# A region of DRAM for each expert's rows, the experts between superblocks 4 and 5, and one maximum over two banks

## The reference

```python
x  = L0_attn_x                                   # (2, 2048, 128)
xn = layernorm(x)
# attention branch, for each batch
s = xn @ W_spin.T + b_spin
scores = (s @ W_J.T) @ s.T / sqrt(128)           # 2048 x 2048
local = softmax(scores) @ s
attn = tanh(beta * (s + mean(s) @ W_global.T + local))
# expert branch, for each token
logits = xn @ Wg.T + bg                          # 16 experts
rw = softmax(top 2 of the logits)
gate, up = (xn @ Wgu[e] + bgu[e])[::2], [1::2]   # gate <= 7, up within +-7
out = sum over the 2 experts of rw * ((up + 1) * gate * sigmoid(1.702 * gate)) @ Wd[e] + bd[e]
result = x + attn + out
```

## Time and profile before

| | us |
|---|---|
| median of 3 runs | 362.35 (361.89 to 365.35) |
| profiled execution | 362.15 |
| its span, first to last instruction | 360.4 |
| busy: PE / DVE / ACT / POOL | 324.9 / 309.9 / 256.8 / 203.7 |
| clock granted to TensorE, mean | 0.981 of 2.4 GHz |

### The profile page before, as it was taken

One profiled execution on the slowest core, in us unless ns is written; L12 is line 12 of the kernel. 1 busy time (PEld: TensorE's weight loads), 2 busy tenths in 40 slices (PEclk: granted clock), 3 DMA queues, 4 the chain that ended last, 5 costly groups with the idle time before them and its releaser, 6 DMA issues.

```text
span 360.4 us, 5972 instructions
## 1 busy us (share of the span) xinstructions
PE 324.9 (90%) x1778; PEld 271.9 (75%) x1779; DVE 309.9 (86%) x630; ACT 256.8 (71%) x509; POOL 203.7 (57%) x271
## 2 busy tenths in 40 slices
PE   1878999998999999999978999999899998989980
PEld 1666788776777778888768999999788786867750
DVE  5988979999978999999769999888878999987855
ACT  2754777876699797687646988888787586578751
POOL 4276851325777777777113444534137777777760
PEclk9978999999999999999999999999999999999996
DMA  5999710000111211212222877765543354555551
GB/s 148 325 332 340 282 35 0 1 31 7 51 51 54 80 46 53 90 51 82 74 87 75 241 222 229 235 207 178 178 117 107 104 164 123 131 145 133 133 126 34
DMA packets 41359, 45.97 MB, mean 128 GB/s; under 512 B 3770, under 2 KB 33082, under 8 KB 41330
## 3 DMA queue, kind: packets, MB, share of 16 engines
q1 hardware_dynamic: 36162, 32.94, 29.1%
q0 software_dynamic: 5168, 12.67, 12.4%
HBM read 23.46 MB, written 22.12 MB: 126 GB/s over the span
## 4 chain that ended last, share of the span: by engine, by line
PE 40%; DVE 22%; POOL 19%; issue 8%; ACT 5%; DMA 4%; POOLq 0%; SPq 0%; ACTq 0%; DVEq 0%
POOL made L547 9%; POOL gy L547 8%; PE PS L556 8%; PE PS L558 8%; PE PS L557 8%; DVE mx L1121 6%; DVE pl L1106 5%; PE PS L609 4%; PE PS L661 2%; PE PS L786 2%; PE PS L771 2%; DVE stats L1077 2%; DMA xy<-slots_x 1%; PE PS L788 1%; PE PS L791 1%
## 5 line engine op out<-in xcount | busy, mean ns | idle before, releaser
L921 ACT ACTIVATE PS<-PS 128x512 f32<-128x512 f32 x128 | 74.8, 585 | 42.8 <-PE PS L558 41.2
L1106 DVE TENSOR_TENSOR pl<-PS,ph 128x512 fp32r<-128x512 f32 x128 | 87.7, 685 | 14.1 <-ACT ph L932 13.5
L1121 DVE TENSOR_REDUCE mx<-PS 128x1 f32<-128x512 f32 x128 | 84.3, 682 | 6.0 <-PE PS L609 6.0
L932 ACT ACTIVATE ph<-PS 128x512 fp32r<-128x512 f32 x128 | 76.5, 598 | 12.1 <-PE PS L558 0.8
L517 POOL DMA_INDIRECT slots_x<-xn,posu x64 | 63.0, 985 | 19.7 <-issue 17.1
L609 PE MATMUL PS<-xT,gq 128*128 128x512 f32 x128 | 49.5, 423 | 6.6 <-DVE mx L1121 6.3
L556 PE MATMUL PS<-gq,xT 128*128 128x512 f32 x128 | 52.4, 410 | 1.5 <-ACT gq L937 0.8
L556 PE MATMUL PS<-ph,rows 128*128 128x512 f32 x128 | 51.5, 402 | 1.8 <-DVE pl L1106 1.8
L558 PE MATMUL PS<-gq,xT 128*128 128x512 f32 x128 | 50.1, 391 | 0.0
L558 PE MATMUL PS<-ph,rows 128*128 128x512 f32 x128 | 50.1, 391 | 0.0
L557 PE MATMUL PS<-pl,rows 128*128 128x512 f32 x128 | 50.0, 391 | 0.0
(11 more groups left out here) (199 smaller groups left out, 682.8 us busy)
## 6 DMA issues: line engine op xcount, KB each, us to landing
slots_y<-yr SPq DMA_DIRECT2D x20, 512.0 KB, 3.1
slots_x<-xs SPq DMA_DIRECT2D x1, 5120.0 KB, 22.0
xy<-slots_x SPq DMA_DIRECT2D x20, 256.0 KB, 3.0
xn<-in_L_attn_x SPq DMA_DIRECT2D x8, 256.0 KB, 5.5
w_f<-in_L_ffn_Wgu SPq DMA_DIRECT2D x1, 2048.0 KB, 12.8
late<-in_L_ffn_Wgu SPq DMA_DIRECT2D x1, 2048.0 KB, 18.3
xs<-in_L_attn_x SPq DMA_DIRECT2D x8, 256.0 KB, 3.5
out_y<-made SPq DMA_DIRECT2D x7, 256.0 KB, 3.3
```

The costliest lines, as they stand in the source:

```text
L921: A(S[:, n % 3], S[:, n % 3], ACT.Exp).then_inc(exp_done, 1)
L932: A(ph[:, i % RING], S[:, n % 3], ACT.Copy).then_inc(s_hi, 1)
L1106: v.tensor_tensor(dst, S[:, n % 3], high.bitcast(F32), ALU.subtract).then_inc(s_lo, 1)
L1121: v.tensor_reduce(mx4[:, a, c:c + 1], MX[:, n % 2], AX.X, ALU.max).then_inc(mx_free, 1)
```

## The change

- Each expert has a region of its own in `slots_x` and `slots_y`, 33 tiles (`ETILES`), so a row number needs only the ranks within the tokens counted so far. Routing is done in two halves of 2048 tokens: choices, shares, `count_pairs`, `ranks`, `places` and the scatter of the first half, then of the second. `tile_list` then makes the list of the 80 tiles: first the whole tiles that the first half has filled, then the others.
- A row of `slots_x` has 129 numbers, the weight last; `xn` likewise. The column of ones in `xy` needs no restoring. Zeros are written only behind the regions and behind each expert's last row (16 transfers).
- SP loads and stores each of a group's four tiles with a transfer of its own, whose row it reads from the list `tile_of` (`rows_at`); its loop is written out. The buffers `xs` of the tokens now serve as `xy`.
- `MOE_AT` is 64: the experts stand between superblocks (numbered from 0) 3 and 4. `oT_part` goes.
- The maxima of superblocks 1 to 7 are made two products at a time (`maxima_pair`) into both banks of `MX`, and reduced by one instruction over 1024 numbers (`maximum_pair`), in two of three steps.
- `add_parts` moves from VectorE to POOL, behind the gathers of the next superblock.

The diff, cut to its core:

```diff
-    MOE_AT = 5 * TB - 4
+    MOE_AT = 4 * TB
+    ETILES = NT + 1
+    REGION = ETILES * P
+    ROWS = (NE * ETILES + NE) * P
...
-        GLOBAL_AT = {12: 0, 14: 1}
-        COUNT_AT = {16: 0, 17: 1}
+        GLOBAL_AT = {16: 0, 28: 1}
+        COUNT_AT = {13: 0, 19: 1}
...
+        def pair_at(j):
+            return 2 * (j // 3) + j % 3 if j < 12 and j % 3 < 2 else None
...
+                sp.wait_ge(pads_ready, 1)
+                for n in range(0, NE, 4):
+                    for row in rows_at(pad_i[0:1, n:n + 4]):
+                        sp.dma_start(slots_x[bass.ds(row, P)], zer[:]).then_inc(pads, 16)
...
-                    sp.dma_start(xy[:, u], slots_x_v[:, bass.ds(4 * g + 8, 4)]).then_inc(xg_in[u], 16)
+                def group_in(g):
+                    for a, row in enumerate(rows_at(tile_of[:, 1, 4 * g:4 * g + 4])):
+                        sp.dma_start(xy[:, g % 2, a], slots_x[bass.ds(row, P)]).then_inc(xg_in[g % 2], 16)
...
-                    sp.dma_start(slots_y_v[:, bass.ds(4 * g - 8, 4)], yr[:, u]).then_inc(y_out[u], 16)
+                    for a, row in enumerate(rows):
+                        sp.dma_start(slots_y[bass.ds(row, P)], yr[:, u, a].bitcast(U32)).then_inc(y_out[u], 16)
...
+                for g in range(2, NG + 2):
+                    if g + 2 <= NG - 3:
+                        rows_in(g + 2)
+                    if g == NG:
+                        sp.wait_ge(t_fill, rows_fill(NG - 1) + 1)
+                        sp.wait_ge(w_kept, NG)
+                        tokens_in(2)
+                    results_out(g)
                     if g < NG:
                         bias_in(g, g % 2)
...
+            def ranks_of(b):
+                pool.wait_ge(e_free, e_no["R", b] + 1)
+                g.tensor_tensor(KEY[:, of(b)], OH1[:, of(b)], RANK[:, of(b)], ALU.mult).then_inc(route_pool, 1)
+                g.tensor_tensor(PROD[:, of(b)], OH2[:, of(b)], RANK[:, of(b)], ALU.mult).then_inc(route_pool, 1)
...
+                        for t in range(part.start, part.stop):
+                            pool.indirect_dma_start(slots_x, bass.IndirectOffsetOnAxis(ap=posu[:, c, t:t + 1], axis=0),
+                                                    xn[:, t], None).then_inc(scat[b][2 if c else q], 16)
+                        if n == 0:
+                            list_consts()
+                            share_one(1)
+                            share_two(1)
+                        if n == 1:
+                            ranks_of(1)
...
+            def maxima_pair(k, q):
+                mx_bank(k, q)
+                a, c = q // 2, 2 * (q % 2)
+                for n in range(2):
+                    m = mm(MX[:, n], gq[:, k % 3, 0, a * P:(a + 1) * P], xT[k // CB][:, 0, 512 * (c + n):512 * (c + n) + 512],
+                           start=True, stop=True)
+                m.then_inc(mx_fill, 1)
...
+            def maximum_pair(k, q):
+                dve.wait_ge(mx_fill, mx_no(k, q) + 1)
+                v.tensor_reduce(mx4[:, q // 2, q % 2:q % 2 + 1], MX.rearrange("p b n -> p (b n)"), AX.X, ALU.max).then_inc(mx_free, 1)
...
+            def places(b):
+                for c in range(2):
+                    dve.wait_ge(route_pool, 4 * b + 3 + c + 2 * (1 - b))
+                    v.tensor_reduce(mk[:, 6, b * TB:b * TB + TB], (KEY, PROD)[c][:, b * TB:b * TB + TB], AX.X, ALU.add).then_inc(dchain, 1)
...
-            ROUTE_AT = {16: 4, 17: 5, 18: 6, 19: 7, 20: 8, 22: 9, 23: 10, 24: 11, 25: 12}
+            SHARE_AT = {13: 0, 22: 1}
+            RANKS_AT = {15: 0, 21: 1}
+            PLACES_AT = {16: 0, 23: 1}
+            LIST_AT = {25: 0, 26: 1, 28: 2, 29: 3}
```

More of the change, by code:

```diff
@@ L308, in _, with rows_at @@
                 sp.dma_start(b_d.rearrange("e (s n) -> e s n", s=2), b_rows[0:NE].bitcast(F32)).then_inc(bd_kept, 16)
+                def rows_at(which):
+                    _, rows = nc.values_load_multi_w_load_instructions(
+                        which, engines=(mybir.EngineType.SP,), min_val=0, max_val=ROWS - P,
+                        skip_runtime_bounds_check_because="the chip's own list of tiles")
+                    return rows
                 def tokens_in(k):
                     if k >= 2:
-                        sp.wait_ge(x_added, k - 1)
-                    sp.dma_start(xs[:, k % 2], x_v[k // CB][:, 4 * (k % CB):4 * (k % CB) + 4]).then_inc(ld_x[k], 16)
-                sp.wait_ge(zeroed, 16)
+                        sp.wait_ge(x_added, k - (k > 2))
+                    sp.dma_start(xs[:, k % 2, :, 0:D], x_v[k // CB][:, 4 * (k % CB):4 * (k % CB) + 4]).then_inc(ld_x[k], 16)
                 tokens_in(0)
@@ L571, in mx_bank @@
             def mx_bank(k, q):
[L572 to L579 removed]
+                if k and q < PAIRS:
+                    pe.wait_ge(mx_free, PAIRS * (k + 1) + q)
+                    if q == 0:
+                        pe.wait_ge(cr_done, k)
+                elif k == 0 and q >= 2:
+                    pe.wait_ge(mx_free, q - 1)
+                return MX[:, 0 if k else q % 2]
             pe.wait_ge(consts, 4)
@@ L702, in count_pairs @@
                 o = e_bank("R", k)
-                pe.wait_ge(oh_ready, 2)
-                mm(o, (onesb, tri)[k][:], ohb, start=True, stop=True).then_inc(e_fill, 1)
+                pe.wait_ge(oh_ready, k + 1)
+                for n in range(2):
+                    m = mm(o[:, n * TB * NE:(n + 1) * TB * NE], (onesb, tri)[n][:], ohb[:, k * TB * NE:(k + 1) * TB * NE],
+                           start=True, stop=True)
+                m.then_inc(e_fill, 1)
             def fields(k, h):
@@ L729, in step @@
                 if k + 1 < NSB:
-                    for q in maxima_at(j):
-                        maxima(k + 1, q, q // 4, q % 4)
+                    if pair_at(j) is not None:
+                        maxima_pair(k + 1, pair_at(j))
                     if j == 13:
@@ L973, in step @@
                     spins_out(*use)
-                if j == 2 and k:
+                if j == 2 and k and k != MOE_AT // TB:
                     values_hi(k - 1)
@@ L1307, in step @@
                 if k + 1 < NSB:
-                    for q in maxima_at(j):
-                        maximum(k + 1, q, q // 4, q % 4)
+                    if pair_at(j) is not None:
+                        maximum_pair(k + 1, pair_at(j))
                     if j == 12:
```

465 lines of the change are left out of this document (239 added, 226 removed).

## The result

The changed kernel takes **413.56 us** (median of 4 runs, 411.91 to 414.44), the kernel before 363.55 (4 runs, 361.89 to 365.35): a ratio of 1.137, with an interval of 1.130 to 1.144. It is slower by 50 us. I had forecast 398 with a range of 380 to 412, so direction and places were right and the loss was 14 us larger, just outside the range. The profiled run of the changed kernel took 411.91 us, its span is 409.8.

The account below looks back on a forecast made before the run. The kernel was taken as a chain of phases with TensorE or VectorE full (90 and 86% busy). From about 362 us, 12 + 2 + 1 + 27 + 2 - 4 - 4 = +36 gave 398 us, range 380 to 412.

Parts of the forecast that it names:

- The routing stall: Routing of the second half: POOL's rank products, queued behind sixteen scattered stores, hold up VectorE; +12 us, with +2 and +1 beside it.
- the wait: VectorE's step 23 idles 12 to 14 us for POOL's rank products behind the stores; +12 us, bounds +8 and +16.
- the clock: After VectorE's idle time in routing, TensorE runs at the lower clock for a while; +2 us, bounds 0 and +4.
- the list: Making the list of tiles takes 20 small VectorE operations in steps 25 to 29 instead of five; +1 us, 0 to +3.
- SP's transfers: Experts: SP issues eight transfers per group for two, so a group takes 5.4 us against 3.47; +27 us, +10 to +34.
- The rival that built on it, 371 us: Experts: SP's issues run hidden beside work and only the delay in routing stays; 371 us, chance 0.08.
- cheaper issues: Experts: SP's issues cost 0.40 to 0.47 us each with registers, +11 to +19 us; 382 to 390 us, chance 0.14.
- The low clock among the experts: Experts: TensorE idles and falls to the lower clock, a group's work taking about 6.4 us; 408 us, chance 0.15.
- Around the experts: Beside the experts: first gather starts four issues after the last result, tokens 2 load late; +2 us, 0 to +4.
- Pairs of maxima: Attention: one reduce of 1024 for two of 512 saves VectorE time, `add_parts` goes to POOL; -4 us, bounds -14 and +6.
- The end: Program's end: gathers finish before attention, so VectorE's last sums follow the last low part; -4 us, -4.6 to -2.

Follow-up runs that it names:

- experiment 1: Changed kernel with POOL's two products for the second batch's ranks issued ahead of the second block of eight row stores: 402.91 us, ratio 1.107.
- experiment 3: Kernel before with only the maxima over two banks by one instruction put in: 368.14 us, ratio 1.013.
- experiment 4: Changed kernel with both banks still filled and given back as a pair, but each reduced by its own instruction: 415.48 us, ratio 1.146.
- experiment 10: Kernel before with only `add_parts` moved from VectorE to POOL, between the gathers: 371.88 us, ratio 1.026.
- experiment 6: Kernel before with each expert group's load and store cut into four at fixed rows, without a list: 374.34 us, ratio 1.034.

## Why the forecast was right in its places and 14 us short

1. **The routing stall** was right in its mechanism, and its sum came out by luck. Forecast +15 (12 for the wait, 2 for the clock, 1 for the list), measured +14.3 by step 28. Inside it the terms shifted: the wait and the clock together gave back 10.2 us in experiment 1, the clock 0.3 of them. The rest of the routing cost about 4 (100.59 against 96.53 us without the stall), where I had one: 1.6 us already by step 16, 3.5 by step 22. For the same reason VectorE reached step 23 at 91.5 us, not at 86 to 88, and its wait was 9.8 us, not 12 to 14. It also waited 1.7 us in step 22 for POOL's share (L537), behind the first eight stores, which I had not named.
2. **SP's transfers** were right in kind. Forecast 5.4 us a group and +27; measured 5.48 where nothing is disturbed, and +28.9. What I had not seen is that an issue now and then takes 1.2 to 1.35 us: eleven groups were 3.5 us longer, mostly for it. Between POOL's products of the groups thirteen intervals, not fourteen, became longer, 75.3 us for 45.8, and single ones took 4.2 to 8.0 us; one group too many in my sum and the long issues nearly cancel. The sentence of the Trainium skill in *DMA: Bandwidth & Descriptors*, "Issuing engines are not separate DMA queues", that issue time is usually small relative to the DMA is no guide here: one issue is 0.53 us against 1.9 us to the landing, but eight of them stand in a row on one sequencer. The rival that built on it, 371 us, fell, and so did cheaper issues. The low clock among the experts is half right: the clock fell for part of the time, but the price that I gave it, a group of 6.4 us, was not paid, since the group at 0.50 throughout took 5.46.
3. **Around the experts** I had +2. Without pairs, the steps behind the experts lost 1.9 us, which fits. Between steps 28 and 63 there is 1.0 more without a name; the other parts of this term were not run by themselves.
4. **Pairs of maxima is the step that failed.** I forecast -4 us and bounded a loss by +6; the pairs cost 8.4 in this kernel and 3 to 6 alone in the kernel before. That makes 12 of the 14 us (the other steps, measured against forecast: -0.7, +1.9, +0.9, -0.4). The sum was drawn from VectorE's busy time, where the gain is real (5.8 us fewer) and worth nothing. I had even written that two steps of three would run at 1.85 to 1.9 us because the pair fills both banks, and then set the saved busy time against it. The 19.5 us of waits for the maxima, from which I took that much could be won, were misread too: that answer adds TensorE's weight loads (13.2 us) to its products (6.3 us), which wait at the same time. What bounds these steps is the round trip of a bank: fill, reduce, give back. With one bank at a time TensorE can fill one while the other is reduced; with the pair it waits ahead of the products of the maxima (the table in experiment 3), with one reduce or with two (experiment 4).
5. **The end** was right: -4 forecast, -4.4 measured. The reason was, too: POOL's gathers set the end before (experiment 10), and after it VectorE's last sums waited for none. But it is a gain only for a change that has slack for POOL; `add_parts` on POOL in the old order costs 9.

The sum by what was measured: 14.3 + 28.9 + 7.7 (pairs) + 1.0 + 1.9 - 4.4 = 49.4 us.

## What to carry to other kernels

Cost a queue by its issues, not by its bytes: count the issues of one sequencer in a round of the loop, with what their addresses need, and compare the sum with the round's length; and take out issues before moving them. Double buffers that are filled and freed together are one buffer: a longer instruction that saves its engine time can still cost, if it takes away the overlap of filling and emptying. And work put behind a queue of slow operations on one engine is as late as that queue, so a product that someone waits for goes ahead of the stores that nobody waits for.

## What the runs showed that I had not expected

- An issue at a fixed row was busy for 0.43 us, one at a row from registers for 0.33 plus 0.20 of register work: fixed addresses save almost nothing per issue. What they save is the reading of the row numbers, 0.5 and 0.7 us with the gaps around it per block of four.
- Single issues of SP that took 1.0 to 2.1 us, the longest in experiment 6 (2.11), in every kernel with four issues in a row, whether rows were fixed or not: five of the 178 of the changed kernel's experts took over 0.9 us, none of the 58 before. What they wait for the profile doesn't show.
- On one chip the kernel before took 466.5 us (459.2 to 468.9) instead of 363. With `add_parts` on POOL it took 450.3 there, where that edit costs 9.2 us on the other chip. In the trace of that one ScalarE stood idle for up to 20.2 us at a time between 110 and 180 us, the stretch of POOL's scattered stores, and eight times in the whole run what released it is not in the profile (operation, releaser, us in total, times, longest):

```profile
ACT PS L928 <- remote: 58.8, 8, 14.3
...
ACT PS L928 <- issue: 23.5, 7, 20.2
```

  The cause stays open.
